# Zeroes moved, queries from two queues, a first unit in halves, a group scaled by ScalarE, and six gate chunks sent through memory

## The reference

```
x = LN(x + attention with 16 heads of 64, causal, over 4 x 512 tokens as 16 x 128)
x = LN(x + mixture of 8 experts, ReLU, given gates)
x = LN(x + feed-forward: 2 shared + 16 routed experts, top 2)
x = LN(x + attention with 16 heads of 16, band mask)
x = LN(x + cross attention to ctx, 16 heads of 16)
x = LN(x + 8 experts, GELU, summed, times one gate norm_g of each token)
```

```
out = silu(flat @ wg_s) * (flat @ wu_s) @ wd_s              # 256 hidden columns, shared
comb = top-2 of softmax(flat @ router_w), renormalised       # (tokens, 16)
h = silu(flat @ wg_r) * (flat @ wu_r) * comb[:, :, None]     # 16 experts x 64 hidden columns
out = out + sum over experts of h @ wd_r
```

## Time and profile before

| | us |
|---|---|
| median of 3 runs | 1547.68 (1547.19 to 1548.28) |
| profiled execution, its own time | 1546.91 |
| its span, first to last instruction | 1544.9 |
| PE busy | 1506.9 |
| DVE busy | 993.8 |
| ACT busy | 725.9 |
| POOL busy | 204.4 |

### The profile page before, as it was taken

How to read it: one execution, slowest core, us unless ns; L and a number is a source line. 1 busy time by engine, 2 the same in 40 slices (tenths; PEclk the granted TensorE clock), 3 DMA queues, 4 the chain that set the end, 5 groups by cost and what they waited for, 6 DMA issues and landing times.

```text
span 1544.9 us, 28583 instructions
## 1 busy us (share of the span) xinstructions
PE 1506.9 (98%) x11018; PEld 1311.1 (85%) x11018; DVE 993.8 (64%) x2131; ACT 725.9 (47%) x1874; POOL 204.4 (13%) x215
## 2 busy tenths in 40 slices
PE   7999999999999999998999999999999999999997
PEld 6988998789999999987888877777777989999996
DVE  6777777865544545576666567788887464544447
ACT  4665666622222222222233377788885444444443
POOL 1322232310000000002000033212221200000001
PEclk9999999999999999999999999999999999999999
DMA  6000100011100101000000277678760000000001
GB/s 220 1 15 2 42 2 1 29 40 36 32 28 28 53 27 39 24 11 34 1 14 1 50 103 119 82 102 115 124 97 28 10 19 28 28 27 27 27 0 54
DMA packets 43081, 66.50 MB, mean 43 GB/s; under 512 B 4577, under 2 KB 33505, under 8 KB 42849
## 3 DMA queue, kind: packets, MB, share of 16 engines
q1 hardware_dynamic: 42976, 65.09, 20.3%
HBM read 36.24 MB, written 2.10 MB: 25 GB/s over the span
## 4 chain that ended last, share of the span: by engine, by line
PE 90%; DVE 6%; ACT 2%; issue 1%; DMA 1%; SPq 0%; POOL 0%; DVEq 0%; POOLq 0%; ACTq 0%
PE ps L85 24%; PE ps L86 23%; PE ps L87 23%; PE ps L1880 3%; PE ps L1894 3%; PE ps L392 2%; PE ps L1925 2%; PE ps L1870 2%; PE ps L404 2%; PE ps L417 2%; PE ps L1908 1%; PE ps L1867 1%; ACT wPr L472 1%; PE ps L1916 0%; PE ps L1842 0%
## 5 line engine op out<-in xcount | busy, mean ns | idle before, releaser
L871 ACT ACTIVATE m2hT_h<-ps 128x512 fp32r<-128x512 f32 x128 | 76.8, 600 | 281.2 <-PE ps L87 281.2
L995 DVE TENSOR_TENSOR m6hT_l<-m6h,m6hT_h 128x512 fp32r<-128x512 f32 x128 | 88.6, 692 | 164.8 <-ACT m6hT_h L869 164.7
L997 DVE SCALAR_TENSOR_TENSOR m2hT_l<-ps,m2hT_h 128x512 fp32r<-128x512 f32 x128 | 88.5, 691 | 163.4 <-ACT m2hT_h L871 163.4
L868 ACT ACTIVATE m6h<-ps,m6b 128x512 f32<-128x512 f32 x128 | 88.2, 689 | 197.0 <-PE ps L87 193.0
L2006 ACT ACTIVATE nPr<-ps,negm 128x128 f32<-128x128 f32 x512 | 147.2, 384 | 24.7 <-DVE negm L2109 23.8
L87 PE MATMUL ps<-w_h,m6hT_l 128*128 128x256 f32 x512 | 144.4, 282 | 0.0
L85 PE MATMUL ps<-w_h,m6hT_h 128*128 128x256 f32 x512 | 143.5, 280 | 0.6 <-DVE m6hT_l L995 0.6
L86 PE MATMUL ps<-w_l,m6hT_h 128*128 128x256 f32 x512 | 143.7, 281 | 0.0
L87 PE MATMUL ps<-m2w_h,m2hT_l 128*128 128x256 f32 x448 | 126.8, 283 | 0.0
L86 PE MATMUL ps<-m2w_l,m2hT_h 128*128 128x256 f32 x448 | 126.7, 283 | 0.0
L85 PE MATMUL ps<-m2w_h,m2hT_h 128*128 128x256 f32 x448 | 126.3, 282 | 0.0
(11 more groups left out here) (322 smaller groups left out, 4331.5 us busy)
## 6 DMA issues: line engine op xcount, KB each, us to landing
nKm<-nKc_h SPq DMA_DIRECT2D x64, 128.0 KB, 4.3
nQs<-nQc_h SPq DMA_DIRECT2D x64, 128.0 KB, 5.5
raw<-in_w_e1i SPq DMA_DIRECT2D x9, 512.0 KB, 3.3
raw<-in_w_e1o SPq DMA_DIRECT2D x9, 512.0 KB, 3.3
raw<-in_w_e6i SPq DMA_DIRECT2D x9, 512.0 KB, 3.3
raw<-in_w_e6o SPq DMA_DIRECT2D x9, 512.0 KB, 3.3
nKm<-nKc_l SPq DMA_DIRECT2D x32, 128.0 KB, 4.9
nQs<-nQc_l SPq DMA_DIRECT2D x32, 128.0 KB, 5.5
```

Of the source, the lines that this page charges most:

```text
L868: nc.scalar.activation(c.h32[:, u % 2, :], ps[:, u % 2, :], ACT.Gelu, bias=bias)
L871: nc.scalar.activation(c.hT[0][:, ch, :], ps[:, u % 2, :], ACT.Relu).then_inc(c.s["hi_ready"], 1)
L995: last = nc.vector.tensor_tensor(c.hT[1][:, ch, :], c.h32[:, u % 2, :], c.hT[0][:, ch, :].bitcast(F32), ALU.subtract)
L997: last = nc.vector.scalar_tensor_tensor(c.hT[1][:, ch, :], ps[:, u % 2, :], 0.0, c.hT[0][:, ch, :].bitcast(F32), ALU.max, ALU.subtract)
```

## The change

It has six parts.

1. *First unit in halves*: unit 0 arrives in two transfers of 256 columns (for each of two row blocks), and DVE makes high and low of the first half, then x, then the second half. PE's first fill waits for the first half alone.
2. *Gates by way of memory*: chunks 2 and 3 are still spread by PE (`SL = 4`). For chunks 4 to 9 DVE copies the 16 transposed gate rows to SBUF (`F3.combR`), SP stores them to memory off the chip, and loads two rows for each chunk back, each on 64 partitions, into four buffers `F3.gate`. DVE's gate product reads that buffer in place of a PSUM bank.
3. *Selector*: it is smaller (2 chunks in place of 8), and DVE copies it in group 0 behind the product of chunk 0, not within the mixture.
4. *Zeroes moved*: POOL writes the zeroes and ones behind the first root of the stage, not ahead of it.
5. *Queries from two queues*: three of the first six query transfers are issued by ACT; SP issues the first half's others, then the keys of the second half, then its queries. `fs` moves from step 2 to 3, `fn` from step 4 to 6.
6. *ACT scales a late group*: in M6, group 2 is scaled by ACT as x * rstd - mean * rstd, with the shift made by POOL, behind the last hidden chunk.

```diff
@@ project (first step, PE)
-            if G == 0 and j % 2 == 0:
+            if G == 0 and kind == "q" and j == 0:
+                pe.wait_ge(first_ready, 1)
+            elif G == 0 and (j % 2 == 0 or kind == "q" and j == 1):
                 pe.wait_ge(prep_done, U_A1 + (unit + 1 + j // 2))
@@ mix_scalar
+        if c.gelu:
+            act.wait_ge(c.s["shift"], 2)
+            for j in range((NG - 2) * GB, (NG - 1) * GB):
+                nc.scalar.activation(X[:, j, :], X[:, j, :], ACT.Identity, bias=c.t1[:, j:j + 1],
+                                     scale=rstd[:, j:j + 1]).then_inc(c.s["x_by_act"], 1)
@@ mix_pool
+            if c.gelu and g == NG - 2:
+                nc.gpsimd.tensor_scalar(c.t1[:, own].unsqueeze(2), mv[:, own, 0:1], -1.0, None, ALU.mult).then_inc(c.s["shift"], 1)
+                pool.wait_ge(c.s["shift"], 1)
+                pool.wait_ge(c.s["rstd_ready"], g + 3)
+                nc.gpsimd.tensor_tensor(c.t1[:, own], c.t1[:, own], rstd[:, own], ALU.mult).then_inc(c.s["shift"], 1)
@@ mix_vector, last expert
-                else:
+                elif not c.gelu or u < NU - 1:
                     normalise(q - NG)
@@ ffn_order
-                order += ([("s", c)] if c >= SC else []) + ...
+                order += ([("s", c)] if SC <= c < SL else []) + ...
@@ new: who waits for which gate, which buffer, store and loads
+    def ffn_gated(g, c):
+        if c < SL:
+            return F3.s["g_evac"], ffn_evac(g, ffn_spread(c))
+        return F3.s["gated"], g * (FC - SL) + (c - SL + 1)
+    def ffn_place(c):
+        i = c - SL
+        return (i, 0, 1) if i < 2 else (2 + i % 2, (i - 2) // 2, 2)
+    def ffn_store_gates(sp, g):
+        sp.wait_ge(F3.s["rows_ready"], g + 1)
+        sp.dma_start(gate_rows, F3.combR[0:R_N, :]).then_inc(F3.s["rows_stored"], 16)
+        sp.wait_ge(F3.s["rows_stored"], g * 16 + 16)
+    def ffn_lay_gates(sp, g, chunks):
+        for c in chunks:
+            i, load, _ = ffn_place(c)
+            if load:
+                sp.wait_ge(*ffn_gated(g, c - 2))
+            rows2 = gate_rows[2 * (c - SC):2 * (c - SC) + 2, :]
+            sp.dma_start(F3.gate[i], rows2.unsqueeze(1).broadcast_to([2, R_MID, GT])).then_inc(F3.laid[i], 16)
@@ ffn_sync
-        with sp.Fori(1, NG) as g:
+        sp.wait_ge(s["xt_hi"], DC + C1)
+        sp.dma_start(F3.Xs[:, :, :], X[:, GB:2 * GB, :]).then_inc(s["xs_loaded"], 16)
+        with sp.Fori(2, NG) as g:
             sp.wait_ge(s["xt_hi"], g * DC + C1)
             sp.dma_start(F3.Xs[:, :, :], X[:, bass.ds(g * GB, GB), :]).then_inc(s["xs_loaded"], 16)
+            ffn_store_gates(sp, g - 1)
+            ffn_lay_gates(sp, g - 1, range(SL, FC))
+        ffn_store_gates(sp, NG - 1)
+        ffn_lay_gates(sp, NG - 1, range(SL, FC))
@@ ffn_pool
+        pool.wait_ge(s["ln_var"], 1)
+        root()
         nc.gpsimd.memset(n_Km[0:6 * HD, :, :, :, :].bitcast(F32), 0.0).then_inc(zeroed, 1)
         nc.gpsimd.memset(n_V[:, :, :, :, :], 1.0).then_inc(zeroed, 1)
-        with pool.Fori(0, NG) as g:
+        with pool.Fori(1, NG) as g:
             pool.wait_ge(s["ln_var"], g + 1)
-            nc.gpsimd.tensor_tensor(rstd[:, 0:GB], veps[:, 0:GB], mhalf[:, 0:GB], ALU.pow).then_inc(s["rstd_ready"], 1)
+            root()
@@ product (feed-forward, DVE)
-                v.wait_ge(s["g_full"], ffn_full(g, ffn_spread(g, c)))
+                if c < SL:
+                    v.wait_ge(s["g_full"], ffn_full(g, ffn_spread(c)))
+                    gate, done = ps[:, 4 + c % 2, :], s["g_evac"]
+                else:
+                    i, load, loads = ffn_place(c)
+                    v.wait_ge(F3.laid[i], g * (16 * loads) + 16 * (load + 1))
+                    gate, done = F3.gate[i], s["gated"]
                 v.wait_ge(s["t_done"], g * FC + c + 3)
-                nc.vector.tensor_tensor(F3.h32[:, c % 2, :], F3.tt[:, c % 2, :], ps[:, 4 + c % 2, :], ALU.mult).then_inc(s["g_evac"], 1)
+                nc.vector.tensor_tensor(F3.h32[:, c % 2, :], F3.tt[:, c % 2, :], gate, ALU.mult).then_inc(done, 1)
@@ gates_transposed (DVE)
+            nc.vector.tensor_copy(F3.combR[0:R_N, :], src).then_inc(s["rows_ready"], 1)
             link(nc.vector.tensor_copy(hi, src))
@@ ffn_vector steps, group 0 chunk 0
+                        ffn_selector(v)
@@ n_order_vector
-            order += ... ([("fs", 0)] if n == 2 else []) + ([("fn", 0)] if n == 4 else [])
+            order += ... ([("fs", 0)] if n == 3 else []) + ([("fn", 0)] if n == 6 else [])
@@ n_sync, first group
-                for x in range(2):
-                    sp.wait_ge(s["g_evac"], n_filled(G, NQF + x))
-                    sp.sem_inc(waited_sp, 1)
-                    lay_queries(0, x)
+                sp.wait_ge(s["g_evac"], n_filled(G, NQF))
+                sp.sem_inc(waited_sp, 1)
+                lay_queries(0, 0)
                 lay_keys(0, 1)
+                sp.wait_ge(s["g_evac"], n_filled(G, NQF + 1))
+                sp.sem_inc(waited_sp, 1)
                 lay_queries(1)
@@ n_scalar, ahead of its steps
+        act.wait_ge(s["g_evac"], n_filled(0, NQF + 1))
+        act.sem_inc(waited_act, 1)
+        act.wait_ge(zeroed, 2)
+        n_lay_queries(act, 0, 1)
@@ SP, the attention's units in group 0
                 load_unit(sp, U_A4, k, w_a4[:, at:at + n], n)
+                if k == 1:
+                    ffn_store_gates(sp, 0)
+                    ffn_lay_gates(sp, 0, range(SL, FC - 2))
+                elif k > 1:
+                    ffn_lay_gates(sp, 0, [FC - 4 + k])
@@ DVE, unit 0
-            def high_a1():
-                v.wait_ge(raw_loaded[0], 16)
-                nc.vector.tensor_scalar(wA1[0][:, 0:RAW], raw[0][:, :], 1.0, None, ALU.mult).then_inc(split_hi, 1)
-            def low_first(): ...
+            def first_half(j):
+                w, r0 = [half_unit(t, j) for t in wA1], half_unit(raw[0], j)
+                v.wait_ge(a1_loaded[0] if j else first_loaded, 16)
+                nc.vector.tensor_scalar(w[0], r0, 1.0, None, ALU.mult).then_inc(first_hi, 1)
+                v.wait_ge(first_hi, j + 1)
+                nc.vector.tensor_tensor(w[1], r0, w[0].bitcast(F32), ALU.subtract).then_inc(prep_done if j else first_ready, 1)
```

More of the change, by code:

```diff
@@ L1166, in program @@
     m2 = Region(nc, M2.end, r2.end - M2.end)
-    F3.sel32 = m2.place("f3sel32", [P, FC - SC, P], F32)
-    F3.sel = r1b.place("f3sel", [P, FC - SC, P], F32R)
+    SL = SC + 2
+    F3.sel32 = m2.place("f3sel32", [P, SL - SC, P], F32)
+    n_x0_at = r2.start + 45120
+    assert m.at <= n_x0_at
+    at_x0 = Region(nc, n_x0_at, 8 * KB)
+    F3.sel = at_x0.place("f3sel", [P, SL - SC, P], F32R)
+    at_x0.at = n_x0_at + 2 * KB
+    F3.combR = at_x0.place("f3combR", [P, GT], F32)
+    gates_a = at_x0.place("f3gatesa", [P, 2, GT], F32)
+    gates_b = r1b.place("f3gatesb", [P, 2, GT], F32)
+    F3.gate = [gates_a[:, i, :] for i in range(2)] + [gates_b[:, i, :] for i in range(2)]
+    F3.laid = [sem(f"f3_laid{i}") for i in range(4)]
+    gate_rows = nc.dram_tensor("gate_rows", (R_N, GT), F32).ap()
     F3.s = signals("f3", "xs_loaded xt_hi g_full g_evac soft_exp comb_ready gu_full sg_ready t_done hi_ready h_ready "
-                         "d_full r_done ln_var rstd_ready x_done sel_pool sel_ready")
+                         "d_full r_done ln_var rstd_ready x_done sel_pool sel_ready rows_ready rows_stored gated")
     assert m.at <= n_at
-    FG = 2 + FC - SC + DC
+    FG = 2 + SL - SC + DC
     LO_ROWS = 32
@@ L1191, in ffn_order @@
                 order += x[:1] + k[:1] + ([("nk evac", 0)] if k else []) + [("u", c)] + x[1:] + k[1:]
-                order += ([("s", c)] if c >= SC else []) + ([("nq", 0), ("nq", 1)] if queries else []) + [("t", c)]
+                order += ([("s", c)] if SC <= c < SL else []) + ([("nq", 0), ("nq", 1)] if queries else []) + [("t", c)]
                 order += [("nq evac", 0)] if queries else []
@@ L1221, in ffn_evac @@
         return g * FG + (DC + k + 3)
-    FL, FT, FX = 0, 1, 2 + FC - SC
+    FL, FT, FX = 0, 1, 2 + SL - SC
     def ffn_last(g):
@@ L1254, in ffn_pool, with root @@
         s = F3.s
+        def root():
+            nc.gpsimd.tensor_tensor(rstd[:, 0:GB], veps[:, 0:GB], mhalf[:, 0:GB], ALU.pow).then_inc(s["rstd_ready"], 1)
+        pool.wait_ge(s["ln_var"], 1)
+        root()
         nc.gpsimd.memset(n_Km[0:6 * HD, :, :, :, :].bitcast(F32), 0.0).then_inc(zeroed, 1)
         nc.gpsimd.memset(n_V[:, :, :, :, :], 1.0).then_inc(zeroed, 1)
-        with pool.Fori(0, NG) as g:
+        with pool.Fori(1, NG) as g:
             pool.wait_ge(s["ln_var"], g + 1)
-            nc.gpsimd.tensor_tensor(rstd[:, 0:GB], veps[:, 0:GB], mhalf[:, 0:GB], ALU.pow).then_inc(s["rstd_ready"], 1)
+            root()
     def ffn_tensor_x(pe):
@@ L1303, in spread @@
         def spread(g, c):
-            bank = g_fill(g, ffn_spread(g, c))
-            if ffn_last(g) and c >= FC - 2:
-                pe.wait_ge(N.s["g_evac"], n_filled(0, NK + c - (FC - 2)))
```

(31 more changed lines are left out.)

38 lines of the change are left out of this document (21 added, 17 removed).

## The result

The changed kernel takes **1552.38 us** (1551.19 to 1553.21, 8 runs), against 1547.91 (1545.91 to 1548.72, 8 runs) for the kernel before on the same chip: ratio 1.0029, 95% interval 1.0020 to 1.0038. It is slower, by 4.5 us. The forecast was 1538.7. The profiled execution took 1551.19 (span 1549.4, mean granted clock 0.993), the fastest of the eight.

The account below looks back on a forecast made before the run. PE was taken as the bound, carrying 90% of the chain. Terms summing to -8.95 us took the profiled 1546.91 to 1537.96, plus 0.77 for the median: 1538.7 us; likeliest case 1536.5 to 1541, range 1531.0 to 1541.5.

Parts of the forecast that it names:

- The gates' way: Feed-forward gates stored and reloaded through memory: first gates within 10.4 us, 11 us available, so hidden at no cost.
- Rival (b): Gates late: store and load exceed 11 us and DVE, then PE, wait; at 15 us, 1554.7 us; chance 0.04.
- start: First projection: halving unit 0 lets PE begin sooner, and the last of eight evacuations comes 1.0 earlier; -1.0 us.
- group 0: Feed-forward group 0: memsets moved away end the scaling stall, and six spread products leave PE; -7.65 us.
- group 1: Feed-forward group 1: moved memsets hold DVE's normalisation there, so PE stands 5.6 us; net +5.8 us.
- groups 2 and 3: Feed-forward groups 2 and 3: six spread products fewer each, 12 x 0.23; -2.8 us.
- x transposes: At each feed-forward group's end, x transposes no longer wait for the last spread's bank; -0.4 us.
- first queries: Banded attention: issuing three of six query transfers on ScalarE's queue shortens PE's 2.7 us wait; -0.8 us.
- statistics: Attention steps: taking the last group's statistics a step later spares PE's wait for x's low half; -1.0 us.
- end: Kernel's end: scaling moved to ScalarE lets the last product's combine start 1.15 us sooner; -1.1 us.
- Rival (a): Memsets find nothing to hold in group 1, giving -1.4 instead of +5.8: 1531.5 us; chance 0.18.
- Rival (c): Neighbours absorb the small gains of start, queries, statistics and end: 3.9 less gain, 1542.6 us; chance 0.10.

Follow-up runs that it names:

- experiment 1: Changed kernel with each chunk's gate load made as two halves of 64 partitions in place of one of 2 x 64: 1543.35 us, ratio 0.9973.
- experiment 11: Kernel of experiment 3 with the first weight unit loaded and split whole again: 1536.37 us, ratio 0.9927.
- experiment 5: Kernel of experiment 3 with all six first query transfers back on SP's queue, ahead of the second half's keys: 1534.09 us, ratio 0.9907.
- experiment 9: Kernel of experiment 3 with the last feed-forward group's statistics and normalisation back at attention steps 2 and 4: 1537.37 us, ratio 0.9930.
- experiment 10: Kernel of experiment 3 with the last mixture's group before the last scaled by DVE again: 1536.15 us, ratio 0.9929.
- experiment 3: Changed kernel with gate loads in halves of 64 partitions and the memsets held behind group 0's normalisation: 1535.35 us, ratio 0.9919.
- experiment 7: Kernel of experiment 3 with all first queries on SP's queue and the second half's keys held until they have landed: 1532.78 us, ratio 0.9902.
- experiment 6: Kernel of experiment 3 with first queries still on two queues, but SP holding the second half's keys until they land: 1533.12 us, ratio 0.9904.

## Why the prediction was wrong

The step that failed is "The gates' way", which was put down as "Hidden, at nothing". Its bound, "at most 2.1 + 7.8 + 0.5 for an issue = 10.4 us", was for the first gates, and DVE never waited for those; but it took a load's length from a load of another kind, and looked at the first load alone. With two engines a load needs 5.1 us, and the loads of chunks 4 to 9 are one behind another on the same two, so the lateness adds up to chunks 8 and 9. The text had the other two victims in view and cleared both: "that x lands at 717, wanted at 719" (it landed at 723.5), and a ring with "two pitches, 8.4 us" of room (beside the keys of the attention, issued behind it, one load took 13.96). It cost 9.0 us beside the stall in group 1 (experiment 1), and 11.3 without it (1546.62 against 1535.35). Rival (b) is what happened, near its price but by another mechanism: it had the trip of the first gates exceed 11 us. That its price of 1554.7 lies near the measured time is chance. The trace of before could not warn of it, as it has no such load; the pattern in the diff could.

The other terms, by experiment. Each is read without the late gates:

| term | forecast | measured | from |
|---|---|---|---|
| start | -1.0 | -0.1 in the changed kernel's trace; -1.0 by medians | start; experiment 11 |
| group 0 | -7.65 | -6.4 | table, halves |
| group 1 | +5.8 | +6.0 | table, halves |
| groups 2 and 3 | -2.8 | -1.8 | table, halves |
| x transposes | -0.4 | -0.3 | table, the two later ways |
| first queries | -0.8 | +1.3 by medians | experiment 5 |
| statistics | -1.0 | -1.0 to -2.0 | experiment 9 |
| end | -1.1 | -0.8; -1.1 in the profile | experiment 10 |
| sum | -8.95 | -3.1 to -5.3 | |

The kernel of experiment 1 has them all and is 4.1 us faster than before. The three terms behind group 3 (queries, statistics, end) come to -0.45 in its trace (668.52 against 668.97), where the forecast had -2.9. So the forecast would have missed by 4.6 with the gates in time too, outside its range:

- **The collision was right.** That a memset holds the pointer form of the scaling was argued from the earlier trace rows and is shown: 8.54 and 8.70 us beside memsets, 1.37 without. Rival (a) is out. Moving the memsets in time frees 7.25 us of group 1 (44.01 to 36.76).
- **The spreads were over-valued.** "Six spreads each: 12 x 0.23" counts PE's work as if nothing else were late. 24 spreads gave 2.95 us instead of some 5.5: none in group 0, where DVE sets the pitch, and elsewhere less the copy of the gate rows, of which the text had said "nothing; at worst 0.7 in each group". It costs 0.2 (group 2, 4.63 against 4.44).
- **The queries had the wrong sign.** The bound "+0.6 (keys in front)" named the mechanism and made it too small: 1.3 by medians whose intervals overlap, 1.9 in PE's wait (3.9 against 2.0).
- **The start was over-valued.** PE began at 7.35, earlier than the 7.6 of the forecast, but the reckoning of the eight fills took PE's pace as unchanged, and the quicker pace came later.
- **Rival (c)** is borne out in part: statistics and end kept what they gained, the queries brought a loss, and the start lost most of its gain: in the changed kernel to PE's pace, in that of experiment 3 also to a wait of 0.37 us for an evacuation of the queries.

The best version here is the kernel of experiment 7: gate loads in halves, zeroes behind the normalisation, queries on one queue with the keys behind them, 1532.78 us, ratio 0.9902 (0.9887 to 0.9917). It is not told apart from experiment 6, 1533.12.

## What to carry to other kernels

Before a transfer is called hidden, read the outermost extent of both its patterns, and add up all transfers that go one behind another through the same engines, with the ones queued behind them; the first one's latency says little. When a hold on a shared port is moved, look for the next instruction of the held kind at the new place, and start the holder behind it. Where two defects overlap, mend them together too: one may hide part of the other.
